# Token mixer of a two-layer hybrid model: batches written out, some lag taps as diagonal products, and biases laid over a whole bank by one product

## The chip, the cores and the metric

One Trainium2 chip, one of its cores. TensorE (PE) does the matrix products and transposes, VectorE (DVE), ScalarE (ACT) and GpSimd (POOL) the elementwise work, SyncE issues most of the DMAs. The metric is the device time of one execution in microseconds (us). Before the change it is 1863.72 us, the median of three runs (1859.49 to 1864.86).

## The reference

The program is a chain of eight stages on an array x of 8 batches, 512 tokens and 128 features, in f32: linear attention, mixture of experts, softmax attention, mixture of experts, grouped attention, a quantized feed-forward block, the token mixer, the feed-forward block again. Each adds its output to x. The change touches the first and the seventh. The seventh, cut to what matters:

```python
def mixer(x):                              # called with the layernorm of x, and added to x
    xn = x / (rms(x) + 1e-8)
    u = silu(xn @ Wu.T + bu)               # 256 features
    v = silu(xn @ Wv.T + bv)
    # causal Toeplitz sum over the first axis (the 8 batches), a coefficient for each
    # lag and head; the first lag's is "zero", the others are "pos":
    o[n] = sum(coef[lag] * v[n - lag] for lag in range(n + 1))
    return (u * o) @ Wo.T + bo + x         # + x: the mixer's own shortcut
x = x + mixer(layernorm(x))
```

Since layernorm(x) is itself x times a scale plus a shift for each token, both the input of the products and the shortcut can be had from x by one scale and one shift for each token.

## The kernel before

x stays in SBUF, with 128 tokens in the partitions and 4 tiles of 128 x 128 for each batch. A stage is a block in which each engine runs a program of its own; they are tied together by semaphores that count (`Signal.at(n)` is the count after batch n). No scheduler is at work: on each engine instructions run in the order of the code, and a wait holds up all that stands behind it on that engine.

**Mixer, before** (`token_mixer`, L2327). For each batch: DVE takes the statistics (L192, L196); POOL makes of them, by seven small dependent operations on 128 x 4 numbers with three powers among them, 1/std and the rms factor (L216 to L223, L2337 to L2341); DVE applies mean and 1/std (L245, 4 tiles), ACT the rms factor (L253); PE transposes (L275), ACT copies (L283), PE makes the four products for u and v (L2405), ACT applies silu (L2395). POOL adds the normed tiles to x, which is the shortcut (L2383). Then DVE sums the taps: a multiplication for lag 0 (L2442), a multiply-add for each other lag (L2440), for each of two halves of the features (`FEAT`), which is 2 to 16 operations on 128 x 512 for batches 0 to 7; it gates (L2446); PE makes the output product (L2413) and adds the bias, for each of 4 tiles, by a product of ones with a bias row (L2414); DVE adds the result to x (L2430). `batches` calls the front of batch n + 1 ahead of the back of batch n. On POOL the front of a batch waits for the statistics and for nothing of the batch two before but the tiles that ACT normed, which is early.

**Linear attention, before** (`linear_attention`, L286). On PE the body for batch n is: transposes, sums of the batch before, q and kv products (L365, L368, each kv product with a bias product L369 behind it), the quotient's products of the batch before (L384), transposes of the quotient (L390), a wait for ACT's copy, and for each of 4 tiles the output product (L395) and a bias product (L396).

Of the kernel before, what the change touches and what calls it, by code (L numbers as in the profile page):

```python
# [25 lines left out]
P = 128  # L26
# [259 lines left out]
def linear_attention(nc, k):  # L286

    with Stage(nc, "lin") as st:
# [72 lines left out]
        def _(pe):  # L361
            def project(n, p):
                pe.wait_ge(feed.xT_ready.sem, feed.xT_ready.at(n))
                pe.wait_ge(phi.sem, phi.at(n - 1))
                pe.matmul(ps_q, k.WqT, feed.xT[:, p, :], start=True, stop=True).then_inc(q_ready.sem, 1)  # L365
                pe.wait_ge(v_ready.sem, v_ready.at(n - 1))
                for j in range(T):
                    pe.matmul(kv_view[:, j, :], feed.xT[:, p, j * P:(j + 1) * P], k.WkvT, start=True, stop=False)  # L368
                    ins = pe.matmul(kv_view[:, j, :], k.onesb, k.bkv_rows, start=False, stop=True)  # L369
                ins.then_inc(kv_ready.sem, 1)  # L370
# [16 lines left out]
            def output(n, p):  # L387
# [3 lines left out]
                ins.then_inc(q_turned.sem, 1)  # L391
                pe.wait_ge(aT_ready.sem, aT_ready.at(n))
                for j in range(T):
                    o = ps_out[:, j * P:(j + 1) * P]
                    pe.matmul(o, aT[:, p, j * P:(j + 1) * P], k.WoT, start=True, stop=False)  # L395
                    ins = pe.matmul(o, k.onesb, k.bo_rows, start=False, stop=True)  # L396
# [1930 lines left out]
def token_mixer(nc, k, name="mix"):  # L2327

    with Stage(nc, name) as st:
        half = st.sb("half", [P, T], F32)
        minus_one = st.sb("minus_one", [P, T], F32)

        def rms_factor(steps, pool, p):
            ms = norm.ms[:, :]
            steps.did(pool.tensor_tensor(ms, ms, half[:, :], ALU.pow))  # L2337
# [13 lines left out]
        exps = st.counter("exponents")  # L2351
        uv_ready = st.counter("uv_ready", 4, 2)
        silu_ready = st.counter("silu_ready", 4, 1)
        shortcut = st.counter("shortcut_added", 1, 2)
        taps = [st.counter(f"taps{c}", 1) for c in range(FEAT)]
        gated_ready = st.counter("gated_ready", FEAT, 2)
        out_ready = st.counter("out_ready", 1, 2)
        x_added = st.counter("x_added", 1, 2)
        norm.also_read = shortcut
        block = st.block()  # L2360

        def batches(front, back):
            front(0, 0)
            for n in range(B):
                if n + 1 < B:
                    front(n + 1, (n + 1) % 2)
                back(n, n % 2)

        @block.sync
        def _(sp):  # L2370
            st.credit(sp)

        @block.gpsimd
        def _(pool):
            norm.setup(pool)
            pool.memset(half[:, :], 0.5)
            pool.memset(minus_one[:, :], -1.0).then_inc(exps.sem, 1)
            hold(pool, exps.sem, 1)

            def back(n, p):  # L2380
                hold(pool, norm.normed.sem, norm.normed.at(n))
                x = k.x[:, n * T:(n + 1) * T, :]
                pool.tensor_tensor(x, x, norm.out[:, p, :, :], ALU.add).then_inc(shortcut.sem, 1)  # L2383
            batches(lambda n, p: norm.powers(pool, n, p), back)

        @block.scalar
        def _(act):
            def front(n, p):
                feed.scalar(act, n, p, uv_ready, uv_ready.at(n - 2))
                for c in range(2 * FEAT):  # L2390
                    act.wait_ge(uv_ready.sem, uv_ready.at(n, c + 1))
                    if c == 0:
                        act.wait_ge(gated_ready.sem, gated_ready.at(n - 2))
                    to = uT[:, p, c, :] if c < FEAT else vT[:, c - FEAT, n, :]
                    act.activation(to, ps_uv[c], ACT.Silu, bias=k.buv[:, c:c + 1]).then_inc(silu_ready.sem, 1)  # L2395
            batches(front, lambda n, p: None)

        @block.tensor
        def _(pe):
            def front(n, p):  # L2400
                feed.tensor(pe, n, p)
                pe.wait_ge(feed.xT_ready.sem, feed.xT_ready.at(n))
                for c in range(2 * FEAT):
                    pe.wait_ge(silu_ready.sem, silu_ready.at(n - 1, c + 1))
                    pe.matmul(ps_uv[c], k.WuvT[:, c * P:(c + 1) * P], feed.xT[:, p, :], start=True, stop=True).then_inc(uv_ready.sem, 1)  # L2405

            def back(n, p):
                pe.wait_ge(gated_ready.sem, gated_ready.at(n))
                pe.wait_ge(x_added.sem, x_added.at(n - 2))
                for j in range(T):  # L2410
                    o = ps_out[p][:, j * P:(j + 1) * P]
                    for c in range(FEAT):
# [6 lines left out]
        def _(dve):  # L2419
# [12 lines left out]
            def back(n, p):  # L2432
# [14 lines left out]
                if n >= 1:  # L2447
                    add(n - 1, 1 - p)
# [430 lines left out]
```

## Time and profile before

| | |
|---|---|
| median of 3 runs | 1863.72 us |
| the profiled execution's own time | 1868.03 us |
| its span, first to last instruction | 1866.3 us |
| mean granted TensorE clock | 0.841 of full speed (2.4 GHz; the lower level is 1.2 GHz) |
| PE / DVE / ACT / POOL busy | 72% / 58% / 40% / 44% of the span |
| linear attention, from first statistics to last add | 32.7 to about 140 us |
| mixer, from first statistics to last add | 1642.4 to 1747.9 us |

The page names each group of instructions by its line, engine, operation and tiles. The stages follow each other with a barrier between them, so the time of a stage is read from its own first and last instruction, and what limits it from the waits within it. An f32 product shows in the trace as two matrix instructions, a transpose as one. In the timeline, a bracket gives how long the engine had been idle before an instruction and what released it.

### The profile page before, as it was taken

To read this page: it belongs to the slowest core of one execution; us is meant where nothing else is said; L and a number is where in the kernel's file an instruction comes from. 1 tells how busy PE (TensorE), PEld (TensorE's weight loads), DVE (VectorE), ACT (ScalarE), POOL (GpSimd) and SP (SyncE) were. 2 spreads that over 40 slices of the span, in tenths; PEclk is the share of its full clock that TensorE was granted. 3 is DMA by queue.
4 is the path that set the end of the run, shared out by engine and by line. 5 is a ranking of instruction groups with operands and counts; after the bars stand their busy time and mean duration, and the time that the engine had idled before them with its cause. 6 is when DMAs were issued, how large, how long until landed. Compare 5 with 4: busy or idle time off the path is not lost. (4 is left out here: it accounts for less than half of the span.)

```text
span 1866.3 us, 36265 instructions
## 1 busy us (share of the span) xinstructions
PE 1338.2 (72%) x11228; PEld 869.7 (47%) x11229; DVE 1087.7 (58%) x3234; ACT 749.7 (40%) x1222; POOL 827.1 (44%) x1189
## 2 busy tenths in 40 slices
PE   5873249963988888832499638888899976957485
PEld 3652139961233333321499613333355545634364
DVE  2564435545887777343355466675766625759764
ACT  1221113311466666611133116676655543634153
POOL 2105745533233333357455347676644403446242
PEclk9795569985799999955699858998999997978688
DMA  3004122245333222041222400000000000000001
GB/s 102 0 1 126 45 61 68 68 118 128 66 83 80 64 64 64 3 128 43 64 66 68 117 19 1 1 2 1 1 2 2 1 2 1 1 1 1 1 1 45
DMA packets 87713, 79.80 MB, mean 43 GB/s; under 512 B 11792, under 2 KB 77584, under 8 KB 87281
## 3 DMA queue, kind: packets, MB, share of 16 engines
q1 hardware_dynamic: 76898, 57.16, 12.0%
q0 software_dynamic: 8704, 17.97, 2.9%
q10 hardware_dynamic: 1980, 3.00, 0.8%
q8 instruction: 73, 1.20, 0.3%
q14 instruction: 58, 0.47, 0.1%
HBM read 46.07 MB, written 32.01 MB: 42 GB/s over the span
## 5 line engine op out<-in xcount | busy, mean ns | idle before, releaser
L1146 ACT ACTIVATE grp_pt<-ps 128x1024 f32<-128x1024 f32 (+2 forms) x320 | 244.6, 799 | 213.6 <-PE ps L1223 135.2
L2035 DVE TENSOR_REDUCE soft_mx<-ps 128x2 f32<-128x1024 f32 (+3 forms) x256 | 201.8, 820 | 58.8 <-PE ps L1873 57.5
L680 POOL DMA_INDIRECT products<-moe_product,moe_rows_in x144 | 153.2, 1064 | 148.2 <-DVE moe_product L852 143.4
L1759 ACT ACTIVATE soft_pt<-ps 128x768 f32<-128x768 f32 (+1 forms) x192 | 166.3, 884 | 83.4 <-PE ps L1904 81.8
L1680 POOL TENSOR_SCALAR_AFFINE_SELECT soft_pt<-soft_pt 128x256 f32<-128x256 f32 (+1 forms) x192 | 92.7, 483 | 210.8 <-ACT soft_pt L1759 210.2
L707 ACT ACTIVATE moe_hid<-ps 128x512 f32<-128x512 f32 x144 | 86.0, 597 | 246.3 <-PE ps L744 246.3
L744 PE MATMUL ps<-moe_rT,moe_W_now 128*128 128x128 f32 x1152 | 157.1, 281 | 1.7 <-issue 1.5
L1243 PE MATMUL ps<-grp_pt,grp_vpad 128*32 128x160 f32 (+4 forms) x2048 | 146.1, 394 | 15.8 <-POOL grp_pt L1088 15.7
L753 PE MATMUL ps<-moe_W,moe_hid 128*128 x1152 | 154.8, 278 | 0.0
L658 POOL DMA_INDIRECT sorted_rows<-moe_row,moe_target x128 | 124.8, 975 | 50.2 <-issue 34.6
L744 PEld LDWEIGHTS ps<-moe_rT,moe_W_now 128*128 128x128 f32 x1152 | 143.3, 196 | 4.7 <-issue 4.6
L753 PEld LDWEIGHTS ps<-moe_W,moe_hid 128*128 128x128 f32 x1152 | 140.6, 193 | 1.5 <-issue 0.4
L1088 POOL TENSOR_SCALAR_AFFINE_SELECT grp_pt<-grp_pt 128x256 f32<-128x256 f32 (+1 forms) x192 | 103.1, 545 | 71.5 <-ACT grp_pt L1146 70.6
L1223 PE MATMUL ps<-grp_qst,grp_kst 32*128 32x160 f16 (+4 forms) x1024 | 96.6, 279 | 8.0 <-ACT grp_pt L1146 5.7
L848 DVE COPY moe_W_now<-moe_W 128x512 f32 x144 | 62.0, 431 | 68.7 <-issue 68.7
L275 PE MATMUL ps<-pack,moe_normed 128*128 128x128 f32 x64 | 17.8, 433 | 108.2 <-DVE moe_normed L245 108.2
L852 DVE TENSOR_SCALAR moe_product<-ps,moe_rows_in 128x128 f32<-128x128 f32 x144 | 50.5, 351 | 71.9 <-PE ps L753 71.7
L1921 PE MATMUL ps<-soft_pt,soft_vpad 128*32 128x512 f32 (+3 forms) x1024 | 89.7, 445 | 2.0 <-POOL soft_pt L1680 1.9
L1868 PE MATMUL ps<-soft_kst,soft_qst 64*128 64x512 bf16 (+3 forms) x512 | 72.4, 322 | 21.7 <-ACT soft_pt L1759 12.7
L737 PE MATMUL ps<-pack,moe_rows_in 128*128 128x128 f32 x144 | 40.6, 282 | 61.8 <-DMA moe_rows_in<-sorted_rows 61.3
L1243 PEld LDWEIGHTS ps<-grp_pt,grp_vpad 128*32 128x32 f32 x2048 | 51.9, 112 | 61.7 <-POOL grp_pt L1088 23.9
L1223 PEld LDWEIGHTS ps<-grp_qst,grp_kst 32*128 32x128 f16 x1024 | 34.3, 93 | 90.8 <-ACT grp_pt L1146 46.1
(333 smaller groups left out, 2808.5 us busy)
## 6 DMA issues: line engine op xcount, KB each, us to landing
moe_rows_in<-sorted_rows SPq DMA_DIRECT2D x144, 65.0 KB, 1.8
moe_back<-products SPq DMA_DIRECT2D x16, 512.0 KB, 7.2
soft_kst<-soft_scratch_k SPq DMA_DIRECT2D x32, 192.0 KB
moe_W<-in_W SPq DMA_DIRECT2D x2, 2048.0 KB, 8.4
moe_W<-in_W SPq DMA_DIRECT2D x16, 256.0 KB, 7.0
soft_scratch_q<-soft_parts SPq DMA_DIRECT2D x16, 192.0 KB, 2.7
soft_qst<-soft_scratch_q SPq DMA_DIRECT2D x32, 96.0 KB
soft_scratch_k<-soft_parts SPq DMA_DIRECT2D x14, 192.0 KB, 2.7
```

The source lines that it names most:

```text
L658: pool.indirect_dma_start(k.sorted_rows, bass.IndirectOffsetOnAxis(target[:, p, s, j:j + 1], 0), row[:, p, j, s, :], None).then_inc(scatte ...
L680: pool.indirect_dma_start(k.products, bass.IndirectOffsetOnAxis(rows_in[:, u, DEST_COL:DEST_COL + 1].bitcast(U32), 0), product[:, u, :], N ...
L744: ins = pe.matmul(ps_hid[u % 2][:, c * P:(c + 1) * P], W1_now[:, u % 2, c * P:(c + 1) * P], rT[:, u % 2, :], start=True, stop=True)
L753: ins = pe.matmul(ps_out[u % 2][:, 0:P], hid[:, u % 2, c * P:(c + 1) * P], W2[:, bass.ds(e, 1), c * P:(c + 1) * P].rearrange("f a h -> f ( ...
L1088: pool.affine_select(e, e, [[0, 2 if seg < 2 else 4], [1, P]], ALU.is_ge, 0.0, 0, -1).then_inc(kept.sem, 1)
L1146: act.activation(at.pair(pt[:, s % 2, :], pair, seg)[:, :, 0:w], ring[(chunks_before(m) + c) % 2][:, :, 0:w], ACT.Exp, scale=scale).then_i ...
L1223: ins = pe.matmul(ring[now % 2][:, b, col:col + w], kst[32 * g:32 * g + 32, p, j * P:(j + 1) * P], qst[32 * g:32 * g + 32, p, s, j * P:j * ...
L1243: ins = pe.matmul(sums[half][32 * g:32 * g + 32, q:q + w], vpad[:, p, j, par, g, :], at.head(pt[:, s % 2, :], g, seg, a, w), start=(par == ...
L1680: pool.affine_select(e, e, [[0, 2 if seg < 2 else 4], [1, P]], ALU.is_ge, 0.0, 0, -1).then_inc(kept.sem, 1)
L1759: act.activation(LATENT.pair(pt[:, s % 2, :], pair, seg)[:, :, 0:w], ring[second_turn(n, c) % RING3][:, :, 0:w], ACT.Exp, scale=scale).the ...
L1921: ins = pe.matmul(sums[half][32 * g:32 * g + 32, q:q + w], vpad[:, n % 2, par, j, 4 * half + g, :], LATENT.head(pt[:, s % 2, :], g, seg, a ...
L2035: ins = dve.tensor_reduce(mx[:, tile, half, :, r], ring[first_turn(n, d) % RING3][:, :, at:at + keys], AX.X, ALU.max)
```

## The change

In the mixer all engines' programs are written anew, with plain loops over the 8 batches:

- POOL makes, by twelve operations a batch (ten of them dependent), a scale and a shift for the products' input and a scale and a shift for the shortcut. It also builds, after batch 0's, six diagonal matrices: the identity times a lag's coefficients.
- ACT makes the products' input from x (`entries`, 4 tiles, scale and shift) and, after the silus of a batch, applies the shortcut to x in place (`shortcuts`, 4 tiles). DVE and POOL no longer do either.
- PE takes 0, 0, 1, 1, 2, 2, 2 and 3 lags of batches 0 to 7 (`PE_LAGS`) as products of a diagonal matrix and v, summed in a bank of PSUM; DVE's first tap of such a batch adds that bank.
- v's products and silus come before u's; each half of the features is gated and multiplied on its own.
- The output's bias is laid over the whole bank by one product of 512 columns ahead of the output products. In linear attention the kv biases are laid by two such products ahead of the kv products, the output bias by one ahead of the wait for ACT's copy.

```diff
+    PE_LAGS = [[], [], [1], [1], [1, 2], [1, 2], [1, 2], [1, 2, 3]]
+    OUTPUTS = (2, 3, 0, 1)
...
+            def power(n):
+                p = n % 2
+                mean, var = mv[:, p, :, 0], mv[:, p, :, 1]
+                pool.wait_ge(stats_done.sem, stats_done.at(n))
+                need(pool, powered, powered.at(n - 1))
+                need(pool, shortcut, shortcut.at(n - 2))
+                pool.tensor_scalar(tmp[:, :], var, 1e-5, None, ALU.add).then_inc(powered.sem, 1)
...
+                pool.tensor_tensor(in_shift[:, p, :], tmp[:, :], in_scale[:, p, :], ALU.mult).then_inc(powered.sem, 1)
+                pool.tensor_tensor(x_shift[:, p, :], tmp[:, :], rstd[:, :], ALU.mult).then_inc(powered.sem, 1)
+                pool.tensor_scalar(x_scale[:, p, :], rstd[:, :], 1.0, None, ALU.add).then_inc(powered.sem, 1)
...
+            power(0)
+            for c in range(FEAT):
+                for lag in range(1, DIAGS + 1):
+                    at = c * B + lag
+                    ins = pool.tensor_scalar(diag[:, c, lag - 1, :], k.ident, k.coef[:, at:at + 1], None, ALU.mult)
+            ins.then_inc(diags_set.sem, 1)
+            for n in range(1, B):
+                power(n)
...
+            def entries(n):
+                p = n % 2
+                act.wait_ge(powered.sem, powered.at(n))
+                need(act, x_turned, x_turned.at(n - 2))
+                for j in range(T):
+                    ins = act.activation(entry[:, p, j, :], k.x[:, n * T + j, :], ACT.Identity, bias=in_shift[:, p, j:j + 1], scale=in_scale[:, p, j:j + 1])
+                ins.then_inc(normed.sem, 1)
+
+            def shortcuts(n):
+                p = n % 2
+                act.wait_ge(normed.sem, normed.at(n))
+                for j in range(T):
+                    x = k.x[:, n * T + j, :]
+                    ins = act.activation(x, x, ACT.Identity, bias=x_shift[:, p, j:j + 1], scale=x_scale[:, p, j:j + 1])
+                ins.then_inc(shortcut.sem, 1)
...
+            entries(0)
+            copy_xT(0)
+            entries(1)
             for n in range(B):
                 if n + 1 < B:
...
+                    copy_xT(n + 1)
+                silus(n)
+                shortcuts(n)
+                if n + 2 < B:
+                    entries(n + 2)
...
+            def turn(n):
+                pe.wait_ge(normed.sem, normed.at(n))
+                need(pe, xT_ready, xT_ready.at(n - 1))
...
+            def tap(n):
+                turn_of = with_taps.index(n)
+                for c in range(FEAT):
+                    pe.wait_ge(silu_ready.sem, v_ready(n - 1, c))
+                    if turn_of > 0:
+                        pe.wait_ge(taps[c].sem, taps_through(n - 1) + 1)
+                    for i, lag in enumerate(PE_LAGS[n]):
+                        ins = pe.matmul(ps_tap[c], diag[:, c, lag - 1, :], vT[:, c, n - lag, :], start=(i == 0), stop=(i == len(PE_LAGS[n]) - 1))
+                    ins.then_inc(tapped.sem, 1)
+
+            def output(n):
+                need(pe, x_added, x_added.at(n - 1))
+                pe.matmul(ps_out, k.onesb, k.bto_rows.unsqueeze(1).to_broadcast([P, T, P]), start=True, stop=True)
...
+            turn(0)
+            turn(1)
+            project(0)
+            pe.wait_ge(diags_set.sem, 1)
+            for n in range(B):
+                if n + 2 < B:
+                    turn(n + 2)
+                if n + 1 < B:
+                    project(n + 1)
+                if n + 1 in with_taps:
+                    tap(n + 1)
+                output(n)
...
+            for n in range(B):
+                if n + 2 < B:
+                    stats(n + 2)
+                mix(n)
+                gate(n)
+                if n > 0:
+                    add(n - 1)
```

In linear attention:

```diff
-                for j in range(T):
-                    pe.matmul(kv_view[:, j, :], feed.xT[:, p, j * P:(j + 1) * P], k.WkvT, start=True, stop=False)
-                    ins = pe.matmul(kv_view[:, j, :], k.onesb, k.bkv_rows, start=False, stop=True)
+                for b in range(2):
+                    pe.matmul(ps_kv[:, b, :], k.onesb, k.bkv_rows.unsqueeze(1).to_broadcast([P, 2, 2 * P]), start=True, stop=True)
+                for j in range(T):
+                    ins = pe.matmul(kv_view[:, j, :], feed.xT[:, p, j * P:(j + 1) * P], k.WkvT, start=False, stop=True, skip_group_check=True)
```

The order on POOL in the mixer, before, from the last steps for batch 0 to the next batch. The semaphore slots in brackets are shown by the name under which an earlier stage used them.

```order
L2341 TENSOR_TENSOR mix_factor<-mix_ms,mix_minus_one 128x4 [waits moe1_route_steps]
L216 TENSOR_SCALAR mix_power_in<-mix_mv 128x4 [waits moe1_logits_ready,moe1_ranks_ready]
L218 TENSOR_TENSOR mix_rstd<-mix_power_in,mix_minus_half 128x4 [waits moe1_route_steps]
L221 TENSOR_TENSOR mix_ms<-mix_mv,mix_rstd 128x4 [waits moe1_route_steps]
L223 TENSOR_TENSOR mix_ms<-mix_ms,mix_rstd 128x4 [waits moe1_route_steps]
L2337 TENSOR_TENSOR mix_ms<-mix_ms,mix_half 128x4 [waits moe1_route_steps]
```

And now, from the end of batch 1's steps to the start of batch 2's. Here moe1_e2_ready stands for `stats_done`, moe1_gap_ready for `powered`, and moe1_pool_set for `shortcut`.

```order
L2413 TENSOR_TENSOR mix_in_scale<-mix_rstd,mix_factor 128x4 [waits moe1_gap_ready]
L2415 TENSOR_SCALAR mix_tmp<-mix_mv 128x4 [waits moe1_gap_ready]
L2417 TENSOR_TENSOR mix_in_shift<-mix_tmp,mix_in_scale 128x4 [waits moe1_gap_ready]
L2418 TENSOR_TENSOR mix_x_shift<-mix_tmp,mix_rstd 128x4
L2419 TENSOR_SCALAR mix_x_scale<-mix_rstd 128x4
L2399 TENSOR_SCALAR mix_tmp<-mix_mv 128x4 [waits moe1_pool_set,moe1_gap_ready,moe1_e2_ready]
L2401 TENSOR_TENSOR mix_rstd<-mix_tmp,mix_half 128x4 [waits moe1_gap_ready]
```

From batch 2 on the first operation of a batch waits for a third semaphore, the shortcut of the batch two before.

The order on PE in the mixer around the projections of batches 1 and 2, before:

```order
L275 MATMUL ps<-pack,mix_normed 128x128 x4
L2405 MATMUL ps<-mix_xT,pack 128x512 x4
L2413 MATMUL ps<-pack,mix_gated 128x128 x2
L2414 MATMUL ps<-bias_rows,onesb 128x128
L2413 MATMUL ps<-pack,mix_gated 128x128 x2
```

And now (`mix_entry` is the products' input, L2485 the projection, L2494 the taps on PE):

```order
L2478 MATMUL ps<-pack,mix_entry 128x128 x8
L2485 MATMUL ps<-mix_xT,pack 128x512 x4
L2478 MATMUL ps<-pack,mix_entry 128x128 x4
L2485 MATMUL ps<-mix_xT,pack 128x512 x4
L2499 MATMUL ps<-bias_rows,onesb 128x512
L2503 MATMUL ps<-pack,mix_gated 128x128 x8
L2478 MATMUL ps<-pack,mix_entry 128x128 x4
L2485 MATMUL ps<-mix_xT,pack 128x512 x4
L2494 MATMUL ps<-mix_vT,mix_diag 128x512 x2
```

The transposes ahead of a projection are now those of the batch after it; before they were those of the same batch.

## Rows read from the trace of the kernel before

**Rows 1.** Window of the mixer: us, busy PE PEld DVE ACT POOL, PEclk, DMA.
```profile
1642.00:1748.00 106.00, 69.04 (x256) 42.06 (x256) 83.41 (x200) 37.92 (x73) 52.10 (x67) 0.75 0.00 1
```

**Rows 2.** Groups of the mixer: line, count | busy us, mean ns | idle before.
```profile
L2440 DVE SCALAR_TENSOR_TENSOR mix_mixed<-mix_vT,pack,mix_mixed 128x512 f32<-128x512 f32 x56 | 39.7, 777 | 0.0
L245 DVE TENSOR_SCALAR mix_normed<-x,mix_mv,mix_rstd 128x128 f32<-128x128 f32 x32 | 13.0, 465 | 12.8 <-POOL mix_factor L2341 12.8
```

**Rows 3.** Timeline, DVE, the mixer: start, duration, instruction [idle before].
```profile
1642.41 0.87 DVE L192 BATCH_NORM_STATS2 mix_bn<-x 128x6 f32<-128x128 f32 x4 [1.60 <-PEq L112]
...
1732.00 9.35 DVE L2440 SCALAR_TENSOR_TENSOR mix_mixed<-mix_vT,pack,mix_mixed 128x512 f32<-128x512 f32 x14
1741.27 1.28 DVE L2446 TENSOR_TENSOR mix_gated<-mix_mixed,mix_uT 128x512 f32<-128x512 f32 x2
...
1747.17 0.69 DVE L2430 TENSOR_TENSOR x<-ps,x 128x512 f32<-128x512 f32 x1 [4.02 <-PE ps L2414]
```

**Rows 4.** Timeline, POOL, the mixer's powers, of batch 0 and of batch 6.
```profile
1643.85 0.23 POOL L216 TENSOR_SCALAR mix_power_in<-mix_mv 128x4 f32<-128x4 f32 x1 [1.19 <-issue]
1644.16 1.04 POOL L218 TENSOR_TENSOR mix_rstd<-mix_power_in,mix_minus_half 128x4 f32<-128x4 f32 x1
1645.27 0.20 POOL L221 TENSOR_TENSOR mix_ms<-mix_mv,mix_rstd 128x4 f32<-128x4 f32 x1
1645.55 0.20 POOL L223 TENSOR_TENSOR mix_ms<-mix_ms,mix_rstd 128x4 f32<-128x4 f32 x1
...
1647.24 1.04 POOL L2341 TENSOR_TENSOR mix_factor<-mix_ms,mix_minus_one 128x4 f32<-128x4 f32 x1
...
1697.92 0.37 POOL L216 TENSOR_SCALAR mix_power_in<-mix_mv 128x4 f32<-128x4 f32 x1 [2.13 <-DVE mix_mv L196]
...
1704.11 2.13 POOL L2383 TENSOR_TENSOR x<-x,mix_normed 128x512 f32<-128x512 f32 x1
```

**Rows 5.** Groups of POOL: a copy of 128 x 128.
```profile
L1078 POOL COPY grp_vpad<-grp_qkv 128x128 f32<-128x128 f32 x32 | 9.4, 324 | 1.7 <-PE ps L1243 1.7
```

**Rows 6.** Timeline, ACT, the mixer: rms factor on four tiles, then a silu.
```profile
1649.46 1.28 ACT L253 ACTIVATE mix_normed<-mix_normed,mix_factor 128x128 f32<-128x128 f32 x4 [14.82 <-DVE mix_normed L245]
...
1654.70 0.69 ACT L2395 ACTIVATE mix_uT<-ps,pack 128x512 f32<-128x512 f32 x1 [0.86 <-PE ps L2405]
```

**Rows 7.** Groups of ACT, linear attention: 128 x 512 with and without a bias.
```profile
L348 ACT ACTIVATE lin_eq<-ps,pack 128x512 f32<-128x512 f32 x8 | 5.5, 687 | 16.5 <-PE ps L365 16.5
L350 ACT ACTIVATE lin_ek<-ps 128x512 f32<-128x512 f32 x8 | 4.8, 597 | 13.7 <-PE ps L369 13.7
```

**Rows 8.** Timeline, PE, the mixer: transposes and projections.
```profile
1650.79 1.12 PE L275 MATMUL ps<-pack,mix_normed 128*128 128x128 f32 x4 [10.71 <-ACT mix_normed L253]
1652.59 6.55 PE L2405 MATMUL ps<-mix_xT,pack 128*128 128x512 f32 x8 [0.69 <-ACT mix_xT L283]
...
1662.42 6.75 PE L2405 MATMUL ps<-mix_xT,pack 128*128 128x512 f32 x8 [0.69 <-ACT mix_xT L283]
...
1672.47 3.70 PE L2405 MATMUL ps<-mix_xT,pack 128*128 128x512 f32 x8 [0.69 <-ACT mix_xT L283]
...
1687.56 0.66 PE L275 MATMUL ps<-pack,mix_normed 128*128 128x128 f32 x4 [2.22 <-ACT mix_normed L253]
1688.90 5.40 PE L2405 MATMUL ps<-mix_xT,pack 128*128 128x512 f32 x8 [0.69 <-ACT mix_xT L283]
```

**Rows 9.** Timeline, PE, linear attention: output products and the transposes behind them.
```profile
71.76 0.80 PE L395 MATMUL ps<-pack,lin_aT 128*128 128x128 f32 x2 [0.69 <-ACT lin_aT L357]
...
74.37 1.06 PE L275 MATMUL ps<-pack,lin_normed 128*128 128x128 f32 x4
...
110.49 0.49 PE L395 MATMUL ps<-pack,lin_aT 128*128 128x128 f32 x2 [0.77 <-ACT lin_aT L357]
...
111.86 0.61 PE L275 MATMUL ps<-pack,lin_normed 128*128 128x128 f32 x4
```

**Rows 10.** Timeline, DVE, linear attention: the norm that those transposes read.
```profile
110.43 1.12 DVE L245 TENSOR_SCALAR lin_normed<-x,lin_mv,lin_rstd 128x128 f32 x4
```

More of the change, by code:

```diff
@@ L2360, in token_mixer @@
-        block = st.block()
-        def batches(front, back):
-            front(0, 0)
+        exps = st.counter("exponents", 3)
+        diags_set = st.counter("diags_set")
+        stats_done = st.counter("stats_done", 2)
+        powered = st.counter("power_steps", 12)
+        normed = st.counter("normed")
+        shortcut = st.counter("shortcut")
+        x_turned = st.counter("x_turned")
+        xT_ready = st.counter("xT_ready")
+        uv_ready = st.counter("uv_ready", 4)
+        silu_ready = st.counter("silu_ready", 4)
@@ new lines, in token_mixer, with x_of, taps_through, v_ready @@
+        tapped = st.counter("products_tapped", FEAT)
+        taps = [st.counter(f"taps{c}") for c in range(FEAT)]
+        gated_ready = st.counter("gated_ready", FEAT)
+        out_ready = st.counter("out_ready")
+        x_added = st.counter("x_added")
+        block = st.block()
+        def x_of(n):
+            return k.x[:, n * T:(n + 1) * T, :]
+        def taps_through(n):
+            return sum(m + 1 - len(PE_LAGS[m]) for m in range(n))
+        def v_ready(n, c):
+            return silu_ready.at(n, OUTPUTS.index(FEAT + c) + 1)
@@ L2364, in batches @@
             for n in range(B):
                 if n + 1 < B:
[L2366 to L2396, printed above, removed]
+                    copy_xT(n + 1)
@@ L2416, in _, with project @@
-            batches(front, back)
+            def turn(n):
+                pe.wait_ge(normed.sem, normed.at(n))
+                need(pe, xT_ready, xT_ready.at(n - 1))
+                for j in range(T):
+                    ins = pe.transpose(ps_x[:, j * P:(j + 1) * P], entry[:, n % 2, j, :], k.ident)
+                ins.then_inc(x_turned.sem, 1)
+            def project(n):
+                pe.wait_ge(xT_ready.sem, xT_ready.at(n))
+                for i, c in enumerate(OUTPUTS):
+                    need(pe, silu_ready, silu_ready.at(n - 1, i + 1))
+                    pe.matmul(ps_uv[c], k.WuvT[:, c * P:(c + 1) * P], xT[:, n % 2, :], start=True, stop=True).then_inc(uv_ready.sem, 1)
@@ L2427, in add, with gate @@
+            def gate(n):
+                need(dve, out_ready, out_ready.at(n - 2))
+                for c in range(FEAT):
+                    dve.wait_ge(silu_ready.sem, silu_ready.at(n, OUTPUTS.index(c) + 1))
+                    dve.wait_ge(taps[c].sem, counts[c])
+                    dve.tensor_tensor(gated[:, n % 2, c, :], mixed[:, c, :], uT[:, n % 2, c, :], ALU.mult).then_inc(gated_ready.sem, 1)
+            def add(n):
                 dve.wait_ge(out_ready.sem, out_ready.at(n))
                 dve.wait_ge(shortcut.sem, shortcut.at(n))
[L2429 removed]
@@ L2450, in _ @@
-            norm.stats(dve, 0, 0)
-            batches(lambda n, p: feed.vector(dve, n, p), back)
-            add(B - 1, (B - 1) % 2)
+                x = x_of(n).rearrange("p a b -> p (a b)")
+                dve.tensor_tensor(x, ps_out, x, ALU.add).then_inc(x_added.sem, 1)
+            stats(0)
+            stats(1)
+            for n in range(B):
[5 more added lines that the diff above has]
+                    add(n - 1)
@@ L2456 @@
+            add(B - 1)
 PACK = {}
```

149 lines of the change are left out of this document (89 added, 60 removed).

## The prediction

> **What bounds the kernel now.** I read the page's shares first. No engine fills the span, and the stages are separated by barriers, so only two stretches matter: linear attention and the mixer. The window of the mixer shows that in the mixer DVE is the busiest engine, 83.4 of 106 us, PE has 69.0 at a mean granted clock of 0.75, POOL 52.1 [rows 1]. Then the groups: the taps are the largest piece of DVE, and the norm on DVE both costs 13.0 us and waits 12.8 us for POOL's powers [rows 2]. Then the timelines. In the second half DVE runs without a gap (14 taps in 9.35 us, so 0.67 us each), and the end is the last gating, one output product and one add that waits 4.02 us for it [rows 3]. In the first half the mixer is bound by the front's chain: statistics, powers, norm, transposes, projection, silu.
>
> **The change part by part.**
>
> *Taps to PE.* 2 x (1+1+2+2+2+3) = 22 taps leave DVE: 22 x 0.67 = 14.7 us. On PE each is two passes of 512 columns. A projection of eight such passes takes 3.70 us at 2.4 GHz [rows 8], so 0.43 a pass (with 0.27 for the last to come out), and 22 products are 18.9 us there, twice that at 1.2 GHz.
>
> *Norm and shortcut to ACT.* DVE loses 13.0 us of busy time and the 12.8 us of waits behind it [rows 2]; what is left to it is about 58 us. ACT gets two passes over four tiles for each batch instead of one. One is 1.28 us [rows 6]. The new form has a bias. On 128 x 512 a bias costs 0.687 - 0.597 = 0.09 us [rows 7], so four tiles with one cost between 1.28 and 1.64; I take 1.45.
>
> *Powers on POOL.* Twelve operations instead of seven. Undisturbed, a dependent scalar operation takes 0.31 us from start to start, a power 1.11, a product 0.28 [rows 4]. Three powers, four dependent products, three scalar operations and the last two at about 0.22 make 3.33 + 1.12 + 0.93 + 0.43 = 5.8 us, where seven took 1643.85 to 1648.28 = 4.4. Beside DVE's taps the seven took 1697.92 to 1704.11 = 6.2 us [rows 4], 1.4 times as long: 8.1 us for the twelve. These are the two bounds.
>
> The Trainium skill ("SBUF — State Buffer", § Who interferes with whom) says that a DVE instruction with two SBUF inputs, which a tap is, holds the port that POOL reads by, for its whole length. That would charge by the instruction: the seven lost 1.76 us, 0.25 each, so twelve lose 3.0 and take 8.8 us, about 3 us more in the end than by the ratio.
>
> *The new order.* This is the term that decides. POOL's `power(n)` begins with a wait for `shortcut.at(n - 2)`: the shortcut of two batches before, which ACT applies behind that batch's silus. Queued behind it on POOL is everything that batch n needs; ACT's `entries(n)` waits for it, PE's `turn(n)` for that, and PE has `turn(n)` *in front of* `project(n - 1)`. And `project(n - 1)` feeds the silus behind which ACT has `shortcuts(n - 1)`, for which `power(n + 1)` waits. So there is one closed chain a batch, with nothing of it beside the rest:
>
> shortcuts(n) done, power(n+2), entries(n+2), turn(n+2), project(n+1), last silu(n+1), shortcuts(n+1) done.
>
> Its price, power aside: 0.1 for POOL to start, entries 1.45, 0.06 to PE, four transposes 0.85 (1.12 less 0.27) at 1.2 GHz, projection 6.2, 0.04 and silu 0.69, shortcuts 1.45. That is 10.8 us. The clock: PE is idle while POOL and ACT work, from the end of output(n - 1) on, 5 to 7 us a batch (a round of some 17.7 less 0.85, 6.2, one or two pairs of taps at 1.7 and 2.0 of output). Before, the projections behind a long idle time took 6.55 and 6.75 us (1.2 GHz throughout), the one behind 2.22 and 0.69 us of idle 5.40, those in dense work 3.70 [rows 8]. The bounds are 5.4 and 6.8; I take 6.2, nearer the first two as the idle time is longer.
>
> The Trainium skill ("TensorE: Matmul & The Clock Gate", § HAM oscillation) says that idle gaps between bursts bring the clock back to half for the next burst; that speaks against this change. Rows 8 agree, with 3.70 against 6.55.
>
> The powers: for batches 2 and 3 DVE has little to mix, 5.8 and 6.2 us; then more and more of the time lies beside taps, 7.2, 7.6, 8.1 and 8.1. The first five sum to 34.9.
>
> *The start.* power(0) runs from 1643.85 [rows 4] to 1649.65. Behind it stand six diagonals of 128 x 128 at 0.324 [rows 5], 1.9 us, and only then power(1), 5.8: 1657.4. turn(1) is in front of project(0), so entries(1), 1.45, and the transposes, 0.9, come first too: project(0) starts at 1659.75, where it was 1652.59 [rows 8]. It takes 6.55; with silu 0.73 and shortcuts 1.45 the first shortcut is done at 1668.5.
>
> *The loop.* Five rounds: 34.9 + 5 x 10.84 = 89.1, to 1757.6. Then power(7), entries(7), turn(7): 10.6, project(6) from 1768.2, to 1774.4.
>
> *The tail.* Now PE has no wait and is at 2.4 GHz: tap(6) 4 x 0.86 = 3.4, output(5) 0.2 + 16 passes x 0.107 = 1.9, project(7) 3.4, tap(7) 5.1, 0.2 to come out: 1788.4. DVE then has nine taps at 0.67 left, 6.0, gates (0.6 and 0.7), PE the second half of the output, 2.0, DVE the add, 0.7: 1798.4. The old end was 1747.17 + 0.69 = 1747.86 [rows 3]. The mixer loses 50.5 us.
>
> *Linear attention.* The kv biases have as many columns as before, 4 x 256 = 2 x 512, so nothing. The output bias moves into the wait for ACT's copy, which hides it (0.21 or 0.43 us in a gap of over 0.7). Output and biases took 2.61 us at the lower clock (71.76 to 74.37), 1.37 at the higher (110.49 to 111.86) [rows 9]; eight passes alone are 1.71 and 0.86. In three batches at the lower clock that is 0.9 each. At the higher PE would be ready at 111.35, but DVE's norm ends at 111.55 [rows 10], so 0.3 each in the other five. Together 4.2 us, between 1 (none but the slow ones pay, and in part) and 6.
>
> *Bias in the mixer.* It saves PE 0.5 us a batch, which the chain doesn't contain: nothing.
>
> *Sum*, against the profiled execution's own 1868.03 us (span 1866.3): 1868.0 + 50.5 - 4.2 = 1914.3. The median of the runs is 4.3 us below the profiled one, so 1910.
>
> **Rivals.**
>
> *A, the same chain with PE at 2.4 GHz.* If the bursts (8 to 11 us of PE work a round) keep the clock up, transposes cost 0.43 and projections 3.70: 2.9 less in six rounds, 17.5 us: 1892. For it speaks that PE would be busy more than half of each round; against it, that the first two projections stayed low although only 3 us lay between them [rows 8].
>
> *B, the same chain with other sizes of POOL and ACT.* Powers at 5.8 throughout, ACT at 1.28, projections 5.4: about 8 + 2 + 5 less, 1895. Powers at 8.8, ACT at 1.64, projections 6.8: about 8 + 2 + 4 more, 1924.
>
> *C, faster: the wait is met when it is asked for, and the batches overlap.* It decides at one point: if shortcuts(n) were done before stats(n + 2), the powers would run beside the mix and PE would set the pace. At 2.4 GHz it needs 8 x 3.4 + 6 x 0.4 + 18.9 + 8 x 1.9 = 64 us from project(0) at 1659.75, to 1724, and about 10 of last taps and output: 1734, 14 us before the old end. With linear attention: 1846. For it speaks that DVE's load falls by a third; against it, that statistics are cheap and early and silus late, so the wait can't be met. Even with every term of the chain at its least (5.8, 1.28, 0.43, 3.70) a round is 13.4 us and the mixer ends over 20 us later than before.
>
> *D, no gain or loss to speak of*: PE or DVE give back in overlap what the start loses. It needs a round of about 9.5 us, as C does, and has the same against it.
>
> **How the numbers follow.** Forecast 0.65, A 0.13, B's ends beyond the forecast's own range 0.16, C 0.04, D 0.02. The forecast's bounds are those of B, 1895 to 1924; the range takes in A: 1890 to 1926. A measurement of this kernel can tell about 0.3% (5.6 us) from no change. Faster by more than that: 0.04; within: 0.02; slower: 0.94.
>
> **What would show it.** Right: POOL's first operation of batches 2 to 7 (L2399) idle before it with ACT's shortcut (L2445) as releaser; ACT's `entries` (L2437) waiting for POOL; PE's transposes (L2478) idle 5 to 7 us for ACT; projections six times some 17 to 19 us apart; the mixer's clock about as low as before, though DVE is busy for only some 60 of 155 us. project(0) at about 1660. Wrong: projections less than 13 us apart, DVE or PE without gaps in the mixer. Linear attention ends 1 to 6 us earlier, or that step is wrong.

## The result and the profile after

The changed kernel takes 1907.49 us (median of 4 runs, 1906.4 to 1908.63), the kernel before beside it 1864.26 us (1859.49 to 1864.86): 1.0238 times as long, 95% interval 1.0219 to 1.0256. Forecast were 1910 us and a range of 1890 to 1926. The profiled execution took 1907.19 us (span 1905.1).

| | before | after | difference | forecast |
|---|---|---|---|---|
| linear attention, first statistics to those of the next stage | 110.4 | 97.3 | -13.1 | -4.2 |
| mixer, first statistics to end of last add | 105.5 | 156.5 | +51.0 | +50.5 |
| the profiled execution | 1868.0 | 1907.2 | +39.2 | +46.3 |

The window of the mixer after (columns as in [rows 1]): DVE has fallen from 83.4 to 58.0 us, in a stage that is half as long again. No engine is busy for much more than half of it.

```profile
1630.00:1787.00 157.00, 86.05 (x276) 48.87 (x276) 57.95 (x138) 53.49 (x105) 51.01 (x105) 0.73 0.00 0
```

The view of waits, same stretch (who waited <- for whom: us in total, times, longest):

```profile
ACT mix_entry L2437 <- POOL mix_x_scale L2419: 63.9, 8, 14.9
POOL mix_tmp L2399 <- ACT x L2445: 62.8, 6, 11.1
DVE mix_mixed L2549 <- PE ps L2494: 61.9, 10, 13.9
PE ps L2478 <- ACT mix_entry L2437: 56.0, 7, 11.2
```

ACT waits for POOL, POOL for ACT, PE for ACT and DVE for PE, each about 60 us. Engines that take turns for equal times are one chain. POOL, ACT and PE are in it; PE hands back to ACT through the silus, which follow the projection piece by piece and so wait little. DVE only hangs on it: from batch 3 on its statistics were done 9.9 to 16.5 us before POOL's powers started. `POOL <- ACT x` six times is the wait `shortcut.at(n - 2)` of batches 2 to 7. A round of it, POOL's and ACT's timelines, from batch 2's powers on:

```profile
1657.12 0.22 POOL L2399 TENSOR_SCALAR mix_tmp<-mix_mv 128x4 f32<-128x4 f32 x1 [10.47 <-ACT x L2445]
...
1710.32 1.79 POOL L2405 TENSOR_TENSOR mix_tmp<-mix_tmp,mix_rstd 128x4 f32<-128x4 f32 x1
...
1729.87 2.59 POOL L2411 TENSOR_TENSOR mix_factor<-mix_tmp,mix_half 128x4 f32<-128x4 f32 x1
```

```profile
1655.30 1.63 ACT L2445 ACTIVATE x<-x,mix_x_shift,mix_x_scale 128x128 f32<-128x128 f32 x4
1662.94 1.65 ACT L2437 ACTIVATE mix_entry<-x,mix_in_shift,mix_in_scale 128x128 f32<-128x128 f32 x4 [6.00 <-POOL mix_x_scale L2419]
...
1671.97 1.64 ACT L2445 ACTIVATE x<-x,mix_x_shift,mix_x_scale 128x128 f32<-128x128 f32 x4
1679.48 1.65 ACT L2437 ACTIVATE mix_entry<-x,mix_in_shift,mix_in_scale 128x128 f32<-128x128 f32 x4 [5.87 <-POOL mix_x_scale L2419]
```

And PE's, with the last round and the end; these answer to [rows 8]:

```profile
1649.30 5.38 PE L2485 MATMUL ps<-mix_xT,pack 128*128 128x512 f32 x8
1664.69 1.09 PE L2478 MATMUL ps<-pack,mix_entry 128*128 128x128 f32 x4 [10.01 <-issue]
1665.57 5.78 PE L2485 MATMUL ps<-mix_xT,pack 128*128 128x512 f32 x8
...
1681.18 1.12 PE L2478 MATMUL ps<-pack,mix_entry 128*128 128x128 f32 x4 [7.83 <-ACT mix_entry L2437]
1682.09 6.05 PE L2485 MATMUL ps<-mix_xT,pack 128*128 128x512 f32 x8
...
1736.34 4.54 PE L2485 MATMUL ps<-mix_xT,pack 128*128 128x512 f32 x8
...
1753.99 5.94 PE L2485 MATMUL ps<-mix_xT,pack 128*128 128x512 f32 x8
...
1781.97 0.61 PE L2499 MATMUL ps<-bias_rows,onesb 128*128 128x512 bf16 x1 [6.02 <-DVE x L2566]
1782.37 3.62 PE L2503 MATMUL ps<-pack,mix_gated 128*128 128x128 f32 x16
```

From shortcuts(0), done at 1656.93, all follows in the order that the prediction listed: powers, entries, transposes, projection, silus, shortcuts. The projections start 16.3, 16.5, 17.9, 18.5, 17.8 and 17.7 us apart.

Linear attention, by windows of 10 us (columns as in [rows 1]; the last but two is the granted clock). Before:

```profile
62.00:72.00 10.00, 7.39 (x38) 5.88 (x37) 5.38 (x13) 2.97 (x5) 1.26 (x2) 0.84 0.00 0
72.00:82.00 10.00, 9.74 (x46) 7.95 (x46) 4.65 (x17) 2.37 (x4) 1.26 (x2) 0.70 0.00 0
82.00:92.00 10.00, 7.56 (x31) 6.31 (x32) 5.88 (x20) 1.19 (x2) 1.26 (x2) 0.66 0.00 0
```

After:

```profile
62.00:72.00 10.00, 7.56 (x46) 5.87 (x45) 7.11 (x23) 2.97 (x5) 1.27 (x2) 1.00 0.00 0
72.00:82.00 10.00, 7.52 (x45) 5.82 (x45) 7.14 (x23) 2.97 (x5) 1.27 (x2) 1.00 0.00 0
82.00:92.00 10.00, 7.56 (x46) 5.87 (x45) 7.19 (x22) 2.92 (x5) 1.27 (x2) 1.00 0.00 0
```

PE is as busy as before, but completes 46 matrix instructions where it completed 31 in the lowest window: the clock is 1.00 instead of 0.66.

### The profile page after: what moved, and what is told of

Read it like the earlier page. It is cut to its first block and busy times, and to the rows that moved or that the text cites. A ratio compares the mean times of both kernels' runs of the same rounds, so it can differ in the third digit from the quotient of the medians.

```text
span 1905.1 us, 36260 instructions
## 1 busy us (share of the span) xinstructions
PE 1342.2 (70%) x11208; PEld 866.5 (45%) x11209; DVE 1063.5 (56%) x3172; ACT 765.9 (40%) x1254; POOL 828.4 (43%) x1227
## 5 line engine op out<-in xcount | busy, mean ns | idle before, releaser
L2035 DVE TENSOR_REDUCE soft_mx<-ps 128x2 f32<-128x1024 f32 (+3 forms) x256 | 201.9, 821 | 57.0 <-PE ps L1873 55.7
L275 PE MATMUL ps<-pack,moe_normed 128*128 128x128 f32 x64 | 17.8, 433 | 108.5 <-DVE moe_normed L245 108.5
L852 DVE TENSOR_SCALAR moe_product<-ps,moe_rows_in 128x128 f32<-128x128 f32 x144 | 50.5, 351 | 74.1 <-PE ps L753 71.9
```

Source lines behind the costliest of these rows:

```text
L2035: ins = dve.tensor_reduce(mx[:, tile, half, :, r], ring[first_turn(n, d) % RING3][:, :, at:at + keys], AX.X, ALU.max)
```

## The experiments

A ratio is to the median of the kernel before, run beside the version: 1866.91 us for 1, 3, 4 and 5, 1862.97 for 2, 6, 7 and 8, 1864.31 for 9 to 12. "Stage" is the mixer from its first statistics to the end of its last add: 105.5 before, 156.5 after.

**1. Linear attention alone**, and **2. mixer alone.**

```diff
 # 1: the kernel before, with the new linear_attention
 # 2: the new kernel, with the old linear_attention
```

> The kernel before with the new linear attention alone; the mixer is the old one. Forecast's step: linear attention gains about 4 us by fewer instructions behind ACT's copy, so 1860 where before has 1864. The changed kernel's profile shows that stage 13.0 us shorter than before's (32.7 to 143.1 against 32.5 to 129.8), at a granted clock of 0.92 against 0.86. Theory L1: 4 to 5 us of it are the instructions, the rest is where the low clock happened to fall in one execution; then the runs lie at 1857 to 1861. Theory L2: the new order itself keeps the clock up; then the runs lie at 1850 to 1853, and the stage takes 97 to 99 us in this profile too.

> The kernel before with the new mixer alone, the old linear attention. The mixer's loss in the two profiles is 51 us, so 1864 + 51 = 1915 if the two parts are independent, and 8 to 11 us above the changed kernel's 1907. Its profile is a second sample of the old linear attention: near 110 us if the new order itself keeps the clock up there, anywhere from 100 to 110 if the clock fell by chance in the profile of before.

1: 1855.45 us, ratio 0.9939 (0.9915 to 0.9964), linear attention 97.3 us. 2: 1918.92 us, 1.0282 (1.0248 to 1.0315), linear attention 110.0, mixer 157.2. 1 lies between the two theories by its time, and its stage is what L2 said; 2 is 4 us above its forecast. The halves are what the two traces said: some 52 to 56 us lost in the mixer, 9 to 13 won in linear attention. That gain is no accident of one execution: the old order shows 110.4 and 110.0, the new one 97.3 to 101.6 in ten traces.

**3. Is it that chain? PE's order.**

```diff
-                if n + 2 < B:
-                    turn(n + 2)
                 if n + 1 < B:
                     project(n + 1)
+                if n + 2 < B:
+                    turn(n + 2)
```

> The changed kernel with one change in PE's order: the projection of batch n+1 stands ahead of the transposes of batch n+2, POOL's wait stays. Chain theory: the projection leaves the chain, but ACT still has entries(n+2) and the copy ahead of the silus of batch n+1; a round is power 5.7 to 8.1, entries 1.65, transposes and copy 1.8, four silus 2.8, shortcuts 1.64: about 14.8 us where it is 17.4, so about 1892. Rival (the projection alone is the price of the order, the batches overlap without it): 1865 to 1875.

1888.32 us, 1.0116 (1.0097 to 1.0136), stage 136.5: 20 us won. The powers still wait for the shortcut (six times), but project(n + 1) is no longer behind them. As expected of the chain; the rival is 13 us off.

**4. The wait itself.**

```diff
# x_scale and x_shift are indexed by n % 3
-        x_scale = st.sb("x_scale", [P, 2, T], F32)
-        x_shift = st.sb("x_shift", [P, 2, T], F32)
+        x_scale = st.sb("x_scale", [P, 3, T], F32)
+        x_shift = st.sb("x_shift", [P, 3, T], F32)
...
-                need(pool, shortcut, shortcut.at(n - 2))
+                need(pool, normed, normed.at(n - 2))
+                need(pool, shortcut, shortcut.at(n - 3))
```

> The changed kernel with three buffers instead of two for the shortcut's scale and shift, so that POOL's powers of a batch wait for the shortcut of three batches before (and for the products' input of two before) instead of two before. Chain theory: power drops out of the closed chain. A round is then ACT's entries 1.65, transposes 0.85 or 0.43, projection 3.7 to 5.5, silu 0.7, shortcuts 1.64: 8.3 to 10.4 us, or what PE or DVE need, about 9; six rounds at 17.4 become six at about 9.3: 1855 to 1868, and POOL's first operation of a batch no longer waits 10 us for ACT. Rival (PE's work with the taps, or its clock, is what costs, and POOL's wait is only where the slack shows): little changes, 1895 to 1910, and POOL's wait moves to another engine.

1872.08 us, 1.0035 (1.0013 to 1.0057), stage 119.9: 35 us won by one more buffer of two times 4 numbers for each partition, and still 4 us short of what I expected. POOL's timeline tells why:

```profile
1691.22 0.22 POOL L2400 TENSOR_SCALAR mix_tmp<-mix_mv 128x4 f32<-128x4 f32 x1 [1.48 <-DVE mix_mv L2533]
...
1707.90 0.22 POOL L2400 TENSOR_SCALAR mix_tmp<-mix_mv 128x4 f32<-128x4 f32 x1 [11.03 <-DVE mix_mv L2533]
```

The next wait is DVE's: stats(n + 2) stand behind mix, gate and add of earlier batches. It holds POOL up six times. Two projections still follow 7.9 us apart (1671.38, 1679.32), but for the entries of batches 5 and 7 PE waits 4.8 and 5.9 us.

**5. All loosened at once but the statistics.**

```diff
 # 3 and 4 together, and on ACT:
+                if n + 2 < B:
+                    entries(n + 2)
                 silus(n)
                 shortcuts(n)
-                if n + 2 < B:
-                    entries(n + 2)
 # power(1) ahead of the diagonals, project(0) ahead of turn(1)
```

> The three-buffer kernel with three orders changed as well: the projection ahead of the next batch's transposes, ACT's entries(n+2) ahead of silus(n), the diagonals built behind power(1) instead of ahead of it and projection 0 ahead of transposes 1. Chain theory: no closed chain is left, and PE sets the pace (8 x 3.4 + 6 x 0.4 + 18.9 + 8 x 1.9 = 64 us at 2.4 GHz, more where the clock is low); with a start of 11 to 15 us and a tail of 12 the mixer takes 90 to 98 us where before takes 105: 1843 to 1855 with linear attention's gain. Rival (DVE, POOL or ACT bind at about 10 us a batch): 1860 to 1870.

A miss: 1876.34 us, 1.0066 (1.0038 to 1.0093), stage 122.7, so no better than 4. I had closed a new ring. With entries(n + 2) ahead of silus(n) on ACT, the silus wait for the powers, these for the statistics, these on DVE stand behind the mix, which waits for earlier silus. Each round POOL waits the same time for DVE:

```profile
1673.36 0.22 POOL L2400 TENSOR_SCALAR mix_tmp<-mix_mv 128x4 f32<-128x4 f32 x1 [6.78 <-DVE mix_mv L2534]
1685.79 0.22 POOL L2400 TENSOR_SCALAR mix_tmp<-mix_mv 128x4 f32<-128x4 f32 x1 [6.78 <-DVE mix_mv L2534]
1698.62 0.22 POOL L2400 TENSOR_SCALAR mix_tmp<-mix_mv 128x4 f32<-128x4 f32 x1 [6.78 <-DVE mix_mv L2534]
```

**6. Statistics first**, in the changed kernel with nothing else moved, and **7. with an early start.**

```diff
# mv, in_scale, in_shift, x_scale, x_shift for B batches, not 2
-                need(pool, shortcut, shortcut.at(n - 2))
...
-                need(dve, powered, powered.at(n - 2))
...
-            stats(0)
-            stats(1)
+            for n in range(B):
+                stats(n)
             for n in range(B):
-                if n + 2 < B:
-                    stats(n + 2)
                 mix(n)
 # 7: power(1) ahead of the diagonals, project(0) ahead of turn(1)
```

> The changed kernel with scales, shifts and statistics kept for all 8 batches and DVE taking all statistics at the start; POOL waits for nothing but them. The three-buffer kernel still showed ACT waiting 4.6 and 7.3 us for POOL, and POOL waiting for DVE's statistics behind the taps, and in the woven kernel this wait stood in every round (6.8 us). Two-chain theory: the wait for the shortcut was the first closed chain, the statistics behind the taps the second; without both, rounds are 8 to 10 us, and the mixer takes about 107 us: 1857 to 1863. Rival (PE at a low clock or ACT with its doubled norm work is the second bound): no better than the three-buffer kernel, 1868 to 1875.

> The stats-first kernel with the diagonals built behind power(1) instead of ahead of it, and projection 0 ahead of transposes 1. The start theory (diagonals 3.5 us and the wait for entries(1) delay the first projection by what the forecast said): the mixer becomes 4 to 9 us shorter than in the stats-first kernel: 1850 to 1857. Rival (the pace is set later, by PE and DVE, and the start is caught up): less than 2 us.

6: 1854.31 us, 0.9938 (0.9907 to 0.9969), stage 103.4: from 156.5, with the taps, the bias and ACT's two passes all as they were. So those cost nothing like 50 us; the wait did, and with it gone the late statistics, which 6 takes away in the same step. 7: 1851.45 us, 0.9928 (0.9903 to 0.9953), stage 101.0. 6 is 3 us better than expected. 7 has its time in the range, but its stage is only 2.4 us shorter than that of 6, where 4 to 9 were expected and less than 2 by the rival: most of the earlier start is caught up later. Now PE sets the pace. Its timeline in 6:

```profile
1687.34 0.66 PE L2477 MATMUL ps<-pack,mix_entry 128*128 128x128 f32 x4
1687.83 3.60 PE L2484 MATMUL ps<-mix_xT,pack 128*128 128x512 f32 x8
1691.27 3.60 PE L2493 MATMUL ps<-mix_vT,mix_diag 128*128 128x512 f32 x8
1694.70 0.38 PE L2498 MATMUL ps<-bias_rows,onesb 128*128 128x512 bf16 x1
1694.91 1.95 PE L2502 MATMUL ps<-pack,mix_gated 128*128 128x128 f32 x16
1696.70 0.60 PE L2477 MATMUL ps<-pack,mix_entry 128*128 128x128 f32 x4
1697.13 3.60 PE L2484 MATMUL ps<-mix_xT,pack 128*128 128x512 f32 x8
```

No bracket: PE has no gap, a round is 9.3 us, and the projection takes 3.60 us, the higher clock, where the ring had it at 4.5 to 6.05. So do all from batch 2 on; the first two, behind 8.2 and 3.9 us of idle time, take 5.42 and 5.29.

**8. What are the taps on PE worth?** Kernel 7 with fewer of them.

```diff
-    PE_LAGS = [[], [], [1], [1], [1, 2], [1, 2], [1, 2], [1, 2, 3]]
+    PE_LAGS = [[], [], [], [], [], [], [], [1]]
```

> The early-start kernel with one lag of the last batch on PE instead of eleven lags of six batches: 20 taps go back to DVE (13.4 us), 17.2 us of PE work go. Theory: with the chains gone PE (64 us at full clock) and DVE (58 us) are near each other, so without the taps DVE has 71 us and sets the pace in the late batches: 5 to 10 us slower than the early-start kernel. Rival (taps on PE only lower the pace, since f32 products take 0.86 us where DVE takes 0.67): equal or faster.

A miss, in sign: 1847.01 us, 0.9909 (0.9875 to 0.9943), stage 95.4, 4 us faster than with 22 taps on PE, where 5 to 10 slower were expected. The intervals of 7 and 8 overlap, so that it is faster at all rests on the stage, 5.6 us shorter in one trace of each. I had charged DVE with 20 taps and forgotten that in 7 it waits for those of PE, as in this row of its timeline:

```profile
1700.15 0.75 DVE L2548 SCALAR_TENSOR_TENSOR mix_mixed<-mix_vT,pack,ps 128x512 f32<-128x512 f32 x1 [2.42 <-PE ps L2494]
```

**9 and 10. Taps only where DVE has no gap.**

```diff
+    PE_LAGS = [[], [], [], [], [], [1], [1], [1, 2]]                 # 9
+    PE_LAGS = [[], [], [], [], [1], [1, 2], [1, 2], [1, 2, 3]]       # 10
```

> The version with statistics first and one tap on PE, but with taps on PE where DVE has no gap any more: one lag of batches 5 and 6, two of batch 7. Of DVE's path in these batches 6 taps go, 6 x 0.67 = 4.0 us; PE gets 6 x 0.86 = 5.2 us where it waits 1.9 to 3.5 us a batch for ACT. If DVE alone sets the end there: mixer 92 to 93.5 us where it was 95.4, run 1843 to 1845.5. If PE's taps come so late that DVE waits for them (as it did for 1.5 us in batch 7): 94.5 to 97 us, run 1846 to 1849.

> As the version with late taps, with one lag of batch 4, two of batches 5 and 6, three of batch 7 on PE: 16 taps where one tap's version had 2. DVE loses another 8 x 0.67 = 5.4 us against the late taps, PE gains 8 x 0.86 = 6.9 us and becomes the engine without gaps in batches 5 to 7. If the two balance: mixer 91 to 93 us, run 1842 to 1845. If PE sets the pace (as with 22 taps, rounds of 9.3): 97 to 100 us, run 1848 to 1851.

9: 1847.54 us, 0.9895 (0.9866 to 0.9923), stage 97.2. 10: 1851.28 us, 0.9935 (0.9908 to 0.9963), stage 99.5. The rival was right both times, to within 0.3 us of its range. DVE in 8, batch 6's taps, and in 9, batches 5 and 6:

```profile
1698.36 0.87 DVE L2551 TENSOR_SCALAR mix_mixed<-mix_vT,pack 128x512 f32<-128x512 f32 x2
1699.15 8.03 DVE L2544 SCALAR_TENSOR_TENSOR mix_mixed<-mix_vT,pack,mix_mixed 128x512 f32<-128x512 f32 x12
```

```profile
1696.04 1.58 DVE L2548 SCALAR_TENSOR_TENSOR mix_mixed<-mix_vT,pack,ps 128x512 f32<-128x512 f32 x2 [6.21 <-PE ps L2494]
...
1704.64 1.40 DVE L2548 SCALAR_TENSOR_TENSOR mix_mixed<-mix_vT,pack,ps 128x512 f32<-128x512 f32 x2
1705.95 6.71 DVE L2544 SCALAR_TENSOR_TENSOR mix_mixed<-mix_vT,pack,mix_mixed 128x512 f32<-128x512 f32 x10
```

Two things. The bank has to be added: lag 0 becomes a multiply-add (1.40 us for the pair) where it was a multiplication (0.87). Batch 6 falls from 8.90 to 8.11 us, 0.4 for each of its two taps, not 0.67, for 0.86 each on PE. And the tap stands behind turn(6), for which PE waits 1.85 us, and behind project(5), so DVE waits 6.2 us. Earlier in PE's order, ahead of project(5), it might pay; that was not tried.

**11 and 12. Why did linear attention win 13 us?** Kernel 1 with one piece undone.

```diff
 # 11
+                pe.wait_ge(aT_ready.sem, aT_ready.at(n))
                 pe.matmul(ps_out, k.onesb, k.bo_rows..., start=True, stop=True)
-                pe.wait_ge(aT_ready.sem, aT_ready.at(n))
 # 12: each kv product followed by its bias product, as before
```

> The kernel before with the new linear attention, but the output's bias product stands behind PE's wait for ACT's copy instead of ahead of it. Instructions are as few as in the new version; what is gone is that a product fills the wait. L1, the gain is in the instructions saved and the hidden bias: the bias costs 0.2 to 0.4 us a batch again, so linear attention takes 99 to 101 us (first statistics to first statistics of the next stage) where the new version took 97.3 to 101.5 and the old one 110.0 and 110.4, and the run is 1 to 3 us above the run with linear attention alone, 1856 to 1860. L2, the product in the wait keeps PE's granted clock up: three or more of the eight batches show output products at 1.9 us or more again, the stage takes 104 to 109 us, and the run 1860 to 1866.

> The kernel before with only the output bias of linear attention changed (one product ahead of the wait); the kv biases stay four short products, each behind its kv product. If the kv biases cost nothing either way, as the prediction had it, linear attention takes 97 to 101 us and the run 1853 to 1858, as with both changed. L3, the kv biases carry part of the gain (four short products between four long ones start one after the other, and the two of 512 columns can run ahead of the transposed input): 102 to 107 us, and the run 1858 to 1863.

11: 1855.39 us, 0.9948 (0.9924 to 0.9972), stage of linear attention 102.2. 12: 1856.62 us, 0.9951 (0.9926 to 0.9976), 100.2. For 12 the forecast holds: the kv biases cost nothing that can be seen. By its stage 11 falls between the two theories; by its time it is no slower than 1 and just below L1's range. Its window by window clock (compare before's 0.70 and 0.66):

```profile
62.00:72.00 10.00, 7.38 (x36) 5.92 (x36) 6.18 (x17) 2.37 (x4) 0.55 (x1) 0.84 0.00 0
72.00:82.00 10.00, 7.31 (x42) 5.91 (x41) 6.11 (x17) 2.97 (x5) 1.27 (x2) 0.95 0.00 0
82.00:92.00 10.00, 7.39 (x46) 5.95 (x45) 7.17 (x23) 2.97 (x5) 1.26 (x2) 1.00 0.00 0
```

The clock is up 20 us earlier than before (1.00 from 82 to 122, before from 102 on) without any product in the wait. So the filled wait is not the cause, or only for the last 1 to 5 us of the stage. What 1, 11 and 12 share is that the output's bias is laid by one product; that this is the cause is inferred from one trace each of 11 and 12.

## Why the prediction was right

*The ring, the term that decides.* Right in every link, and shown: of the stage's 156.5 us, 37 go with the wait (4), 20 with PE's order (3), 53 with the wait and the late statistics (6); these overlap and don't add up. C and D fall with it: they needed the wait to be met. The order alone told this, before any time was known: the wait's partner stood, on ACT, behind something that needed what stood, on POOL, behind the wait.

*Its sizes.* Measured from shortcuts(0) done to the start of project(6): 97.1 us, forecast 99.7. Within it two errors partly cancel, which is luck. ACT's four tiles take 1.65 and 1.63 us, the upper bound, where I took 1.45: +0.4 a round. The projections of batches 1 to 6 take 5.78, 6.05, 5.64, 4.92, 4.54 and 5.94, 5.5 in the mean, where I took 6.2: -0.7 a round. The powers, from POOL's start to ACT's, were 5.8, 5.7, 6.8, 7.8, 7.9 and 8.1, 42.1 in all; forecast 43.0. In B's upper end a sum is wrong: 8.8 in all six rounds is 9.8 more than 43.0, not 8, so B ends at 1926, where the range ends too.

*The powers beside taps.* The ratio of 1.4 held (8.1 us), and the charge for each instruction gave 8.8. But neither says what happens. Batch 7's powers, with DVE beside them:

```profile
1744.41 0.75 DVE L2549 SCALAR_TENSOR_TENSOR mix_mixed<-mix_vT,pack,ps 128x512 f32<-128x512 f32 x1 [0.94 <-PE ps L2494]
1745.08 4.06 DVE L2545 SCALAR_TENSOR_TENSOR mix_mixed<-mix_vT,pack,mix_mixed 128x512 f32<-128x512 f32 x6
1749.05 1.29 DVE L2560 TENSOR_TENSOR mix_gated<-mix_mixed,mix_uT 128x512 f32<-128x512 f32 x2
```

```profile
1745.01 0.20 POOL L2405 TENSOR_TENSOR mix_tmp<-mix_tmp,mix_rstd 128x4 f32<-128x4 f32 x1
1745.29 1.40 POOL L2407 TENSOR_TENSOR mix_tmp<-mix_tmp,mix_half 128x4 f32<-128x4 f32 x1
1746.78 0.46 POOL L2409 TENSOR_SCALAR mix_tmp<-mix_tmp 128x4 f32<-128x4 f32 x1
1747.32 1.39 POOL L2411 TENSOR_TENSOR mix_factor<-mix_tmp,mix_half 128x4 f32<-128x4 f32 x1
1748.79 1.61 POOL L2413 TENSOR_TENSOR mix_in_scale<-mix_rstd,mix_factor 128x4 f32<-128x4 f32 x1
1750.49 0.24 POOL L2415 TENSOR_SCALAR mix_tmp<-mix_mv 128x4 f32<-128x4 f32 x1
```

Undisturbed (batch 0 of the same trace) these six take 0.20, 1.01, 0.23, 1.04, 0.20 and 0.24. Beside the tap that adds the bank, with one input from SBUF and one from PSUM, POOL isn't held. Beside the taps with both inputs in SBUF three operations are 0.2 to 0.4 us longer. L2413 starts just before the two gating products, also with both inputs in SBUF, and ends 0.06 us behind the second: 1.4 us longer. Behind them nothing is held. Batches 5 and 6 are alike (L2405 1.79 instead of 0.20, L2411 2.59 instead of 1.04, both across the gating). The Trainium skill's rule ("SBUF — State Buffer", § Who interferes with whom), that a DVE instruction with two SBUF inputs contends with a POOL instruction that reads SBUF, agrees with this. What failed is its use as an even charge of 0.25 for all twelve: in batches 5 to 7 only three or four of them meet such an instruction, and one of these the gating. That the ratio of seven operations, taken beside taps without a break, held for these is in part luck.

*The clock, rival A.* It didn't come true. PE's transposes were idle before 6.6 to 10.0 us (forecast 5 to 7) and then always took 1.1 us, so 1.2 GHz, and the projection behind them 4.54 to 6.05, which is part at one level and part at the other, where A needed 3.70. More PE work in a round didn't lift it in a regular way: 4.54 and 5.94 both follow a round with four products of taps. The Trainium skill's advice on gaps between bursts ("TensorE: Matmul & The Clock Gate", § HAM oscillation) agrees: without gaps, in 6 from batch 2 on, all are 3.60.

*The start.* shortcuts(0) done 26.7 us after the first statistics, forecast 26.1. The six diagonals took 3.54 us on POOL, 0.59 each, not the 0.324 of a copy [rows 5]; so project(0) started 19.1 us after the first statistics, not 17.3; the first projection at 5.38 instead of 6.55 gave 1.2 of it back.

*The tail.* From project(6)'s end to the end of the last add 26.8 us, forecast 24.0. I had the last output product at 2.0 us, and PE, having waited 6.0 us for DVE, took 3.62. What PE waited for was the add of batch 6 (0.68), and behind it it laid the bias (0.4): both stood ahead of the last output product and weren't in the sum.

*Taps off DVE, 14.7 us.* Too high: adding the bank costs 0.26 (1.40 less 0.87, for two) for each of 12 first taps, 3.1, so 11.6. It changed nothing, since DVE wasn't what the mixer waited for. By its own terms the prediction should have left DVE 83.4 - 14.7 - 13.0 = 55.7 us, not "about 58"; that 58.0 was measured is luck.

*Linear attention, -4.2.* This term was wrong, by its own sign (1 to 6 us; it was 13.1). The place was right (12: the output bias alone does it), the mechanism wasn't. I reckoned with instructions saved and hidden, at the clock as it was in each batch. At equal, full clock the new round is 10.2 us and the old one 10.3, so the instructions bring about 1 us in all. The other 12 go with the clock, which is low for six windows of 10 us before (0.66 to 0.84) and for two after (0.83), and which I took as given. The forecast of the whole still came within 3 us: this term made it 9 too high, and the 4.3 taken off for the profiled execution, which lay above the median of before and 0.3 below it after, made it 4 too low. So the nearness of the whole is in part luck. So is that of the mixer, 51.0 against 50.5: the chain was 2.6 us shorter than forecast, the start 0.6 and the tail 2.8 longer. What exactly keeps the clock up stays open.

## What to carry to other kernels

Before weighing what work a rewrite moves between engines, follow each new wait of a double buffer round: if its partner stands, on its own engine, behind anything that needs what is queued behind the wait, the engines take turns. Here a deeper buffer of a few numbers took 37 us off the stage, and the best version, with no such wait and without most of the moved taps, has a stage about 10 us shorter than before. Loosen a ring wholly or look for the next one: two partial repairs, 4 and 5, took 37 and 34 us off the stage, and the one that left no wait of the kind, 6, took 53. The best versions here, 8 and 9, are about 1% faster than the kernel before, of which linear attention alone is 0.6% (1), and have few or almost none of the taps on PE that the rewrite was built around. Among 6 to 10 the intervals overlap.

## What the runs showed of the hardware

- The granted clock in linear attention follows small differences in PE's program, repeatably: with the old one it was 0.70 and 0.66, and 0.74 and 0.66, at 72 to 92 us in two traces from separate runs. With one output bias product in place of four (12) it was 1.00, and in the ten traces with the kv biases changed too 0.95 to 1.00, but for one window of 0.83.
- A dependent operation of 128 x 4 on POOL takes 0.2 to 0.4 us longer beside DVE's multiply-adds from SBUF, and 1.4 to 1.6 us longer when it starts just before two gating products from SBUF. Beside a multiply-add with one input from PSUM it is not held. In the trace before L2339 is held so (1.66 us, across the gating at 1692.05).
- On POOL, scaling 128 x 128 by a column takes 0.59 us, a copy 0.32 [rows 5]. On ACT, four tiles of 128 x 128 take 1.65 us with scale and bias from a column, 1.28 with a scale alone [rows 6].
